# A causal mask folded into the head products' contraction, with each product cut into two column halves of TensorE

## What is computed

```
scores = jnp.einsum('bthd,bshd->bhts', q, k) / jnp.sqrt(jnp.float32(dh))
causal = jnp.triu(jnp.full((seq, seq), -jnp.inf, dtype=jnp.float32), k=1)
scores = scores + causal[None, None, :, :]
weights = jax.nn.softmax(scores, axis=-1)
out = jnp.einsum('bhts,bshd->bthd', weights, v).reshape(b, seq, d)
```

## Time and profile before

| what | value |
|---|---|
| median of 3 runs | 1893.15 us |
| lowest and highest | 1891.52 and 1894.34 us |
| span of the profiled execution | 1890.0 us |
| time of the profiled execution around its span | not given apart; the median less the span is 3.15 us |
| busy PE, DVE, ACT, POOL | 88%, 80%, 54%, 49% of the span |
| TensorE clock granted, mean | 0.963 of full |

### The profile page before, as it was taken

One profiled execution on the slowest core, in us unless ns is written; L12 is line 12 of the kernel. 1 busy time (PEld: TensorE's weight loads), 2 busy tenths in 40 slices (PEclk: granted clock), 3 DMA queues, 4 the chain that ended last, 5 costly groups with the idle time before them and its releaser, 6 DMA issues.

```text
span 1890.0 us, 34255 instructions
## 1 busy us (share of the span) xinstructions
PE 1668.7 (88%) x12162; PEld 1083.8 (57%) x12269; DVE 1503.1 (80%) x3386; ACT 1020.8 (54%) x1998; POOL 931.3 (49%) x1120
## 2 busy tenths in 40 slices
PE   2466799999999999999999999999999999999876
PEld 1234357565665657565665657565665657565635
DVE  3776879899797979899797979799897979782712
ACT  3243374746556474746556474747556474736252
POOL 4545263646455473646455464637455464632202
PEclk9787799999999999999999999999999999999897
DMA  3001010010101010110102010100102010101000
GB/s 101 0 6 51 7 48 11 25 34 10 55 8 52 13 52 7 34 30 13 52 8 57 8 51 10 36 25 16 48 8 57 8 51 8 39 13 36 22 13 6
DMA packets 66924, 53.39 MB, mean 28 GB/s; under 512 B 8322, under 2 KB 65474, under 8 KB 66754
## 3 DMA queue, kind: packets, MB, share of 16 engines
q1 hardware_dynamic: 63202, 49.55, 9.5%
q10 hardware_dynamic: 3552, 1.65, 0.3%
HBM read 8.44 MB, written 4.19 MB: 7 GB/s over the span
## 4 chain that ended last, share of the span: by engine, by line
PE 49%; DVE 26%; POOL 9%; ACT 6%; issue 4%; SPq 2%; DMA 2%; ACTq 0%; DVEq 0%; POOLq 0%; another core or an unknown queue 0%
PE bank L908 47%; DVE rmax L731 6%; DVE wkb L678 3%; POOL rstd L351 3%; PE bank L904 3%; ACT prob L491 2%; DVE tree L641 2%; DVE stats L632 2%; DVE rmax L728 1%; ACT xd L497 1%; POOL inner L395 1%; DVE prob L811 1%; DMA qh<-part 1%; SPq L325 1%; DVE inner L641 1%
## 5 line engine op out<-in xcount | busy, mean ns | idle before, releaser
L491 ACT ACTIVATE prob<-bank 128x512 f32<-128x512 f32 x640 | 358.6, 596 | 113.8 <-PE bank L908 109.2
L731 DVE TENSOR_REDUCE rmax<-bank 128x1 f32<-128x512 f32 (+2 forms) x768 | 355.1, 505 | 17.9 <-PE bank L908 17.8
L908 PE MATMUL bank<-kh,qh 72*128 72x512 bf16 (+3 forms) x1024 | 264.5, 308 | 28.4 <-DVE rmax L731 20.3
L439 POOL TENSOR_TENSOR prob<-xdT,spread 128x512 f32<-128x512 f32 x128 | 168.0, 1313 | 234.0 <-ACT spread L491 206.6
L908 PE MATMUL bank<-qh,kh 75*128 75x512 bf16 (+3 forms) x1024 | 255.3, 305 | 18.9 <-ACT prob L491 15.7
L908 PE MATMUL bank<-wexpT,prob 128*128 128x128 f32 x2048 | 267.0, 278 | 2.3 <-POOL prob L439 0.7
L908 PEld LDWEIGHTS bank<-wexpT,prob 128*128 128x128 f32 x2048 | 250.0, 192 | 8.9 <-POOL prob L439 0.9
L491 ACT ACTIVATE spread<-bank 128x512 f32<-128x512 f32 x128 | 76.3, 596 | 298.3 <-PE bank L908 244.6
L678 DVE RECIPROCAL wkb<-wkb 128x512 f32<-128x512 f32 x64 | 211.6, 3327 | 0.0
L908 PEld LDWEIGHTS bank<-qh,kh 75*128 75x128 bf16 x1024 | 100.2, 98 | 190.0 <-ACT prob L491 115.8
L347 POOL TENSOR_TENSOR var<-mv,eps_ln 128x4 f32<-128x4 f32 x112 | 33.1, 296 | 339.3 <-DVE mv L637 339.3
(11 more groups left out here) (211 smaller groups left out, 3395.8 us busy)
## 6 DMA issues: line engine op xcount, KB each, us to landing
qh<-part SPq DMA_DIRECT2D x288, 64.0 KB
kh<-part SPq DMA_DIRECT2D x288, 64.0 KB
x<-in_L_attn_x_dram SPq DMA_DIRECT2D x16, 256.0 KB, 2.8
out_dram<-yo SPq DMA_DIRECT2D x16, 256.0 KB, 3.1
qh<-maxT SPq DMA_DIRECT2D x16, 48.0 KB
wk<-in_L_attn_tm_Wk_dram ACTq DMA_DIRECT2D x1, 256.0 KB
wv<-in_L_attn_tm_Wv_dram ACTq DMA_DIRECT2D x1, 256.0 KB
wr<-in_L_attn_tm_Wr_dram ACTq DMA_DIRECT2D x1, 256.0 KB
```

The source lines that it names most:

```text
L439: raised(pool.tensor_tensor(ug[:, e % 4, :], xdT[:, :], spread[e // 2 % 2][:, :], ALU.mult), "ug_side")
L491: raised(act.activation(dst, src, func, **kw), signal)
L731: last = dve.tensor_reduce(rmax[:, j, h:h + 1], S[n % 2][:, col:col + (j + 1) * P], AX_X, ALU.max)
L908: return pe.matmul(out_, w, x, start=start, stop=stop, **kw)
```

## The change

- The mask becomes 33 more rows of contraction (`KMASK` = 32 + 1). The constant rows are made once at the start by POOL in `early` and `ahead`, spread over all heads by two DMAs, and multiplied with the diagonal blocks only: products that touch a diagonal block take `KALL` = 108 rows, the others `KOPEN` = 75. The products with `maskb` and `maskTb` are gone, 128 a batch.
- Each piece is computed as two column halves of 64 of the array, `(0, 0)` and `(0, HALF)`, with an open part and a diagonal part each. That makes four products of a piece where there were two (three for the piece that is a diagonal block alone).
- The rows for the maxima lie first in `qh` and `kh`, and are in the row stage's products too. A 37th DMA a batch in each half of the heads' spreading (`no_maxima`) sets them to zero.
- The four filler steps leave PE's order. The order is else the same.
- On ACT, POOL and PE the waits of a step are written in another order, the one expected last first, so that the step's own instruction holds it. Some waits that an earlier step of the same engine has already covered are gone.

The core of the diff:

```
-KALL = KROWS + PARTS
+KOPEN = PARTS + KROWS
+HALF = P // 2
+PAIRS = HALF // 2
+KMASK = PAIRS + 1
+KALL = KOPEN + KMASK
+HEADS_IN = 16 * (2 * PARTS * PARTS + 1)
...
-MASKED = -1e30
+EARLY = (2.0 ** 45, 2.0 ** -36)
+AHEAD = (-1.0, -2.0 ** 81)
+WALL = -2.0 ** 45
...
-        2:busy_rows0 3:attT 1:xn2T 3:attn_out 2:busy_rows2 2:row0 2:row1 1:cmk0 3:busy_experts2 2:row2 2:row3 1:cmk1 2:row4 3:xdT 1:cmk2 2:row5
+        3:attT 1:xn2T 3:attn_out 2:row0 2:row1 1:cmk0 2:row2 2:row3 1:cmk1 2:row4 3:xdT 1:cmk2 2:row5
...
+                sp.dma_start(qh[0:PARTS, some, :], no_maxima[:, :]).then_inc(sems[("heads_low", "heads_high")[z]], 16)
...
+            for dst, src in ((qh, early), (kh, ahead)):
+                sp.dma_start(dst[KOPEN:KALL, :, :], src[:, :, :].rearrange("r (o j) p -> r o (j p)", o=1).broadcast_to([KMASK, NH, T])).then_inc(setup["masks_in"], 16)
...
-            def move(b, dst, src, after, signal, n=None, func=ACT.Identity, **kw):
+            def move(b, dst, src, after, signal, n=None, func=ACT.Identity, freed=(), **kw):
+
                 until(act, b, after, n)
+                for name, total in freed:
+                    reached(act, name, total)
...
+            def product(to, left, rows, right, columns, depth, h, at=None):
+
+                where = {} if at is None else dict(tile_position=at)
+                return mm(to, left[0:depth, h, rows], right[0:depth, h, columns], skip_group_check=True, **where)
+
             def row_scores(b, n):
...
                 for h, j, col in pieces(n):
+                    first, second = slice(j * P, j * P + HALF), slice(j * P + HALF, (j + 1) * P)
                     to = S[n % 2][:, col:col + (j + 1) * P]
-                    mm(to, qh[0:KROWS, h, j * P:(j + 1) * P], kh[0:KROWS, h, 0:(j + 1) * P], True, False, skip_group_check=True)
-                    last = mm(to[:, j * P:(j + 1) * P], identb[:, :], maskb[:, :], False, True, skip_group_check=True)
+                    if j:
+                        product(to[0:HALF, 0:j * P], qh, first, kh, slice(0, j * P), KOPEN, h, (0, 0))
+                    product(to[HALF:, 0:j * P + HALF], qh, second, kh, slice(0, j * P + HALF), KOPEN, h, (0, HALF))
+                    product(to[0:HALF, j * P:], qh, first, kh, slice(j * P, (j + 1) * P), KALL, h, (0, 0))
+                    last = product(to[HALF:, second], qh, second, kh, second, KALL, h, (0, HALF))
...
-                    mm(to, kh[:, h, i * P:(i + 1) * P], qh[:, h, i * P:T], True, False, skip_group_check=True)
-                    last = mm(to[:, 0:P], identb[:, :], maskTb[:, :], False, True, skip_group_check=True)
+                    product(to[0:HALF, HALF:], kh, first, qh, slice(i * P + HALF, T), KOPEN, h, (0, 0))
+                    if i < J - 1:
+                        product(to[HALF:, P:], kh, second, qh, slice((i + 1) * P, T), KOPEN, h, (0, HALF))
+                    product(to[HALF:, 0:P], kh, second, qh, slice(i * P, (i + 1) * P), KALL, h, (0, HALF))
+                    last = product(to[0:HALF, 0:HALF], kh, first, qh, first, KALL, h, (0, 0))
```

More of the change, by code:

```diff
@@ L180, in build @@
         part = [[sb(f"part{i}{j}", [P, T], BF16) for j in range(PARTS)] for i in range(2)]
+        early, ahead = (part[1][i][0:KMASK, :].rearrange("r (j p) -> r j p", j=2 * J) for i in range(2))
         bias_part = [part[0][i][0:1, :] for i in range(PARTS)]
@@ L303, in spread_heads @@
                 half = slice(z * P // 2, (z + 1) * P // 2)
+                some = slice(z * NH // 2, (z + 1) * NH // 2)
+                sp.dma_start(qh[0:PARTS, some, :], no_maxima[:, :]).then_inc(sems[("heads_low", "heads_high")[z]], 16)
                 for t, dst in enumerate((qh, kh)):
@@ L308, in spread_heads @@
                             r = m * PARTS + o if t == 0 else o * PARTS + m
[L309 removed]
+                            sp.dma_start(dst[PARTS + r:KOPEN:PARTS * PARTS, some, :], part[t][m][half, :]).then_inc(sems[("heads_low", "heads_high")[z]], 16)
             def spread_maxima(b):
                 until(sp, b, "maxT")
[L313 removed]
+                sp.dma_start(qh[0:PARTS, :, :], maxT[:, :]).then_inc(sems["max_in"], 16)
             def store(b):
@@ L433, in gated_input @@
             def gated_input(b, e):
+                if e == NE - 1 and b + 1 < B:
+                    until(pool, b + 1, "max_part")
                 until(pool, b, "spread_out", e // 2 + 1)
@@ L487, in _, with norm @@
                 act.dma_start(dst, src, allow_slow_non_contiguous=True).then_inc(setup["loaded"], 16)
-            def move(b, dst, src, after, signal, n=None, func=ACT.Identity, **kw):
+            def move(b, dst, src, after, signal, n=None, func=ACT.Identity, freed=(), **kw):
                 until(act, b, after, n)
+                for name, total in freed:
+                    reached(act, name, total)
                 raised(act.activation(dst, src, func, **kw), signal)
-            def norm(b, n, dst, t, signal):
+            def norm(b, n, dst, t, signal, freed=()):
                 until(act, b, f"shift{n}")
+                for name, turn in freed:
+                    until(act, turn, name)
                 for j in range(J):
@@ L558, in first_part @@
             def first_part(b, t):
+                if b == 0 and t == 0:
+                    act.wait_ge(setup["masks_in"], 32)
                 until(act, b - 1, "heads_low")
```

152 lines of the change are left out of this document (62 added, 90 removed).

## The result

| | median us | lowest to highest |
|---|---|---|
| before, same chip | 1893.02 | 1891.52 to 1894.34 |
| after | 1991.81 | 1986.01 to 1999.17 |

The ratio is 1.053, with a 95% interval of 1.050 to 1.056: 98.8 us slower. The forecast was 1957 us.

The account below looks back on a forecast made before the run. No engine alone was the bound, but PE decided some 50 us of a 106 us turn. Terms summed to +4.1 us a turn, over 15.5 turns +64 us on 1890, hence 1957 us; range 1850 to 2035.

Parts of the forecast that it names:

- likeliest case: The forecast itself, 1957 us for the whole kernel, with its own range 1915 to 2010 and chance 0.55.
- A change of width costs 0.09 us each way, 64 as well as 32: PE loses 0.09 us entering or leaving narrow strips; 82 added changes, 2.9 us in row and 1.6 in score stretch.
- Halves overlap, the depth is free: On PE, two column halves run beside each other, and depth 108 instead of 72 or 75 costs nothing.
- Unhidden loads, +3.8 us a turn in the two stretches: PE weight loads exposed in row and score stretches: entries 0.8 and 0.75, f32 returns 0.5 and 0.4, inside 0.6 and 0.75.
- The size of mask and halves, +5.2 us a turn ahead of the waits: Over a turn: row stretch +2.8, score stretch +1.3, first stretch +0.3, third +0.2, last two +0.6 us.
- Late waits, -1.1 us a turn: About 20 releases of ACT, POOL and PE on a turn's path, each 0.05 to 0.06 us earlier.
- The fillers, nothing: Removing eight 512-column PE products a batch in the first stretch gains nothing; PE's 3.5 us of idle time covers them.
- a rival with a chance of 0.2: PE's clock falls in the first stretch without fillers: +1 to +4 us a turn, 1975 to 2025 us; chance 0.2.
- The mask DMAs, nothing: At the start, two mask DMAs go out 150 us or so ahead of the first spreading and cost nothing.
- Free changes to 64: Rival: on PE, changes to halves of 64 cost nothing, -4.25 us a turn, 1827 us; chance 0.14.
- halves that do not overlap: Rival: every piece costs PE twice its columns, 17 us more a turn, over 2100 us; chance 0.03.
- The added PE time hides: Rival: PE waits elsewhere and ACT's earlier starts give back more, 1885 to 1903 us; chance 0.08.

Follow-up runs that it names:

- after_fill: Changed kernel with the four filler steps put back in their old places, nothing else; 1953.0 us.
- after_fill_load_w: Changed kernel with fillers back, the second input's load ahead of the mask DMAs, and POOL's `weighted` waits in their old order; 1933.1 us.
- wide_fill_load_w: As after_fill_load_w, but each piece on all 128 columns instead of halves, with the mask as 43 rows of contraction; 1873.7 us.
- before_waits_w: Kernel before with the new order of waits alone, except POOL's step `weighted`, which keeps its old order; 1883.3 us.
- after_load: Changed kernel with the load of the second batch's input issued ahead of the two mask DMAs; 1982.0 us.

## Why the prediction was right and where it was wrong

The direction was right, and both ranges, 1850 to 2035 and the likeliest case's 1915 to 2010, hold the time. The point was 35 us low, and behind it stand larger errors that partly cancel. Over 15.5 turns the mask and the halves were put some 41 us too high (5.2 us a turn, measured 2.58) and the waits 27 us too low (-1.1, measured +0.63); the fillers' 39 us and the load's 9 us were put at nothing. These are +34 us together. That the time fell into the likeliest case's own range is luck: the parts that this case had (mask, halves and waits) come to some 50 of the 98.8 us, and the rest came by ways that it put at nothing.

The measured 98.8 us come apart by the runs so: 38.9 us for the fillers (after less after_fill), 19.9 us for the load and `weighted` together (after_fill less after_fill_load_w), and 39.7 us for the mask, the halves and the other waits (after_fill_load_w less before). (Their sum is 98.5, since the kernel before differs by 0.4 us between the runs.) The last is +49.8 for mask and halves and -10.1 for the waits. The profiled executions of that last pair are 51.8 us apart: 41.2 us lie ahead of the last turn's first `wo` product, and 10.6 behind it, where the forecast had next to nothing.

- **A change of width costs 0.09 us each way, 64 as well as 32.** Right: 0.095 to 0.099 us at every kind of change. It is the cause of the loss in the steady state: without it (wide_fill_load_w) the same mask is faster than before.
- **Halves overlap, the depth is free.** Right; seven products in the time of their 512 columns and 0.04 us, and the version of 118 rows is faster than before.
- **Unhidden loads, +3.8 us a turn in the two stretches.** This is the term that was mis-sized. Entries were put at 0.8 and 0.75 us: entering costs the change's 0.10 us and nothing more that can be seen. By the Trainium skill, "TensorE: Matmul & The Clock Gate", LDWEIGHTS (loading the stationary operand), a load of 64 columns would take an estimated 0.05 us; the trace does not show it at an entry. Inside a visit 0.03 us is lost with four products and 0.06 us with fifteen, where the forecast had 0.05 us for the entry and 0.025 us for each further piece. Returns to f32 were right: the first pass lasts 0.106 us over its columns, where it lasted 0.056 behind a mask product.
- **The size of mask and halves, +5.2 us a turn ahead of the waits.** Measured: +2.58 (after_fill_load_w against before_waits_w). The row stretch (`row17` to `row39`) was put at +2.8 and came to +1.46; the score stretch (`score4` to `score27`) at +1.3, and came to +0.13; the rest at +1.1, and came to +1.0. In the score stretch the parts can be told: the 37 mask products were 1.97 us of columns (2.2 forecast), the 17 added changes cost 1.65 us (1.6), and loads and what products lose between themselves +0.5 us (1.9). So the difference is the loads'. In the row stretch missing records leave the same split open. The number of added changes in a turn was nearly right, 86 for 82.
- **Late waits, -1.1 us a turn.** The sign was wrong: +0.63 us. ACT does start 0.02 us behind PE (the median over before_waits_w's exponentials) where it was 0.08, as forecast, and that and its like are worth -0.42 us; what failed is the step that costed all releases alike and asked only what is queued behind the waiting instruction on its engine, not whom an earlier start shuts out. The swap in `weighted` costs +1.05 us.
- **The fillers, nothing.** Wrong, the largest miss: 39 us. The idle time of the first stretch does hide the fillers' 1.7 us of columns, as the prediction said, but they hold the clock. The prediction had this as a rival with a chance of 0.2, beside the forecast and not in it, at +1 to +4 us a turn; it came to 3.8, near the upper end, and its time, 1975 to 2025, holds the result. It tied the fall to the first stretch; there it is, and a second one came in `read_out`, so that its upper end needed both.
- **The mask DMAs, nothing.** Wrong: +9 us, once. They were compared with the first spreading of heads, put 150 us later, and not with what SP issues right behind them.
- **Rivals.** Free changes to 64 are ruled out by the rows, and so are halves that do not overlap. "The added PE time hides" is ruled out by the time, but what it rests on is real, and the other way round: DVE is so near that the PE time *taken away* hides (wide_fill_load_w).

"Clock 1.00 in the steady state" was named as what would show the prediction right, and "the clock drops in the first stretch of each turn" as what would make it wrong. It did.

## What to carry to other kernels

Count the visits, not the products: cutting a product into column halves keeps its columns, but each time such a unit stands between full-width neighbours it costs 0.2 us of TensorE, against 0.05 us for a mask product saved. Here it never paid: the same mask at full width was 59 us faster. Filler products in idle time are not free to remove; read the granted clock turn by turn with and without them, and look again after every change that thins the work around them. And when an instruction is made to start earlier, or a DMA is put into a queue, ask who starts just behind it: here the order of two waits cost 1.05 us a turn through DVE, and two DMAs that nobody needed for another 100 us cost 9 us through a load.

## What the runs showed of the hardware

- A fall of the clock is not a property of the program alone: one program (after_load) had turns of 108.9 us and turns of 112.6 us in one execution, and its four times spread over 22 us, where those of before spread over 6.
- Filler products act far from where they stand: the low stretch in `read_out`, 78 us behind the nearest filler, went from all but three turns when the fillers came back. Whether one fall brings on the next is open.
- A small DVE sum of 64 columns with two SBUF inputs took 1.32 us in place of 0.23 when a POOL product had begun 0.03 us ahead of it; with the starts the other way round POOL's product took 1.33 us and not 1.27, and DVE lost nothing.
- A change of width costs the same 0.10 us ahead of loads of 32, 64 and 128 columns, so the load of 64 does not show beside it; on the way back to f32 the first pass is longer by another 0.11 us (0.97 us for the two passes of `wk` at 1009.00, where two times 0.43 is 0.86).
